# Spreading a row of B by fp32 transposes of one repeated column, and summing states by accumulating transposes, in a fused conv and selective-scan kernel

## What is computed

```
def step(h, inp):
    u_t, d_t, B_t, C_t = inp
    dA = jnp.exp(d_t[..., None] * A)
    h = dA * h + (d_t * u_t)[..., None] * B_t[:, None, :]
    y = jnp.einsum('bdn,bn->bd', h, C_t)
    return (h, y)
...
y = selective_scan(xs, delta, A, Bm, Cm, D)
y = y * jax.nn.silu(z)
return y @ out_proj_w.T
```

## Time and profile before

| | us |
|---|---|
| runs | 1001.99, 1002.55, 1007.24 (median 1002.55) |
| profiled execution | 998.73, span 996.6 |
| scan steps 0 to 63, first half | 256.6 to 479.9 |
| scan steps 0 to 63, second half | 732.8 to 954.5 |
| busy, share of the span | PE 85%, DVE 82%, ACT 56%, POOL 52% |

### The profile page before, as it was taken

One profiled execution on the slowest core, in us unless ns is written; L12 is line 12 of the kernel. 1 busy time (PEld: TensorE's weight loads), 2 busy tenths in 40 slices (PEclk: granted clock), 3 DMA queues, 4 the chain that ended last, 5 costly groups with the idle time before them and its releaser, 6 DMA issues. The chain is left out here.

```text
span 996.6 us, 8253 instructions
## 1 busy us (share of the span) xinstructions
PE 842.4 (85%) x2747; PEld 419.2 (42%) x2747; DVE 816.1 (82%) x670; ACT 555.7 (56%) x927; POOL 520.1 (52%) x240
## 2 busy tenths in 40 slices
PE   3999998976488898899999999797648889889985
PEld 2444443432144445455545444343214334544643
DVE  6899884476998998998999888447699999899852
ACT  3754231047569886787667333104765878678712
POOL 2016992110488685877211799311046869577740
PEclk8999999997799999999999999898968999999998
DMA  3000000002434453444100000000113544444411
GB/s 103 1 0 0 0 0 1 0 1 73 106 123 173 139 179 131 152 161 148 44 0 6 16 0 0 1 0 1 47 68 105 184 154 176 140 148 164 148 48 22
DMA packets 32870, 73.82 MB, mean 74 GB/s; under 512 B 15544, under 2 KB 15680, under 8 KB 32832
## 3 DMA queue, kind: packets, MB, share of 16 engines
q1 hardware_dynamic: 31424, 72.04, 21.5%
q0 software_dynamic: 320, 1.05, 0.5%
q10 hardware_dynamic: 1088, 0.26, 0.1%
HBM read 70.71 MB, written 2.62 MB: 74 GB/s over the span
## 5 line engine op out<-in xcount | busy, mean ns | idle before, releaser
L333 POOL TENSOR_TENSOR arena<-arena 128x1024 f32<-128x1024 f32 x128 | 305.3, 2391 | 106.6 <-DVE arena L1567 64.3
L1567 DVE TENSOR_TENSOR_SCAN arena<-arena,ps 128x1024 f32<-128x1024 f32 x128 | 289.4, 2280 | 15.9 <-POOL arena L333 8.3
L568 PE MATMUL ps<-arena,mat 128*128 128x512 f32 x512 | 251.7, 615 | 9.1 <-POOL arena L333 8.0
L808 ACT ACTIVATE arena<-arena,Amat 128x1024 f32<-128x1024 f32 x128 | 146.0, 1143 | 86.9 <-DVE arena L1567 83.4
L808 ACT ACTIVATE arena<-arena 128x128 f32<-128x128 f32 (+4 forms) x320 | 131.7, 480 | 106.4 <-DVE arena L1484 75.3
L568 PEld LDWEIGHTS ps<-arena,mat 128*128 128x128 f32 x512 | 95.1, 196 | 90.1 <-issue 67.2
L681 PE MATMUL ps<-arena,mat 128*128 128x512 f32 x240 | 106.3, 592 | 0.0
L535 PE MATMUL ps<-arena,sel 96*128 96x512 bf16 x148 | 48.0, 411 | 61.8 <-DVE arena L1567 52.4
L1562 DVE TENSOR_TENSOR ps<-arena,ps 128x1024 f32<-128x1024 f32 x74 | 89.5, 1210 | 5.7 <-PE ps L535 5.7
L808 ACT ACTIVATE arena<-ps 128x1024 f32<-128x1024 f32 (+2 forms) x58 | 53.6, 937 | 70.5 <-PE ps L409 20.7
L440 PE MATMUL ps<-arena,diag 128*128 128x512 f32 x180 | 80.5, 603 | 2.4 <-DVE ps L1397 2.4
(11 more groups left out here) (177 smaller groups left out, 1242.4 us busy)
## 6 DMA issues: line engine op xcount, KB each, us to landing
arena<-c_rows SPq DMA_DIRECT2D x128, 512.0 KB, 3.8
out<-arena SPq DMA_DIRECT2D x28, 64.0 KB, 2.2
xres<-x POOLq DMA_DIRECT2D x4, 256.0 KB, 5.3
xres<-x SPq DMA_DIRECT2D x4, 256.0 KB, 4.1
convw<-conv_w SPq DMA_DIRECT2D x1, 576.0 KB
c_rows<-ROWS SPq DMA_DIRECT2D x4, 128.0 KB, 1.9
mat<-mats SPq DMA_DIRECT2D x1, 448.0 KB, 3.9
inw<-in_w SPq DMA_DIRECT2D x1, 256.0 KB
```

Of the source, the lines that this page charges most:

```text
L333: tt(HC[s % 2], HS[s % 2], CB[s % 4], ALU.mult).then_inc(S("hc"), 1)
L568: last = mm(half(PS[3], n), ident, half(HC[s % 2], n), start=first, stop=True, skip_group_check=True)
L808: return nc.scalar.activation(out_, in_, func, bias=bias, scale=scale, accum_out=accum_out)
L1567: nc.vector.tensor_tensor_scan(HS[q], DA[q], PS[q][:, :], 0.0, ALU.mult, ALU.add).then_inc(S("scan"), 1)
```

## The change

It touches the Mamba block of both halves.

1. **No bf16 parts.** `first_part`, `middle`, `rest` and `last_part` are gone. B and C of a pair stand in 64 rows (`keep_rows` copies 64). Before the scan TensorE transposes pair 0's rows (`turn_first_rows`) and ScalarE keeps their B (`keep_first_b`) in `BT`. The other pair's B comes as before from `turn_rows`.
2. **A row of B by turns of a repeated column.** `b_rows` makes eight transposes of one fp32 column of `BT`, repeated 128 times, in place of two bf16 matmuls.
3. **State sums by accumulating turns.** For images 0 to 2 of a half (`TURNED`) `sum_of` makes eight transposes of 128x128 that accumulate in `PS[3]`, so y stands transposed; z is projected in that layout by eight matmuls of 128 columns. To give `out_proj` its operand, the gated y is transposed back (`turn_y`) and copied (`keep_y`). Image 3 is summed as before.
4. **More X steps.** From step 9 to 47 three of five are X steps (24 of 39 where 20 were); from 48 on every other one, as before: 31 of 64. The scaled blocks have a third buffer.
5. **Moved.** The pieces of pair 0's end go three steps later (output projection 33/34 to 36/37, last projection 44 to 47, centering 36 to 39, adding the block 46 to 49, and so on), and its result tile and store move. At the end of the first half two empty matmuls (`write_all`) open `PS[0]` and `PS[1]` before `first_tap`.

```diff
-            d["BCS"] = d["BCS"][:, 0:L // 2].bitcast(bf16)
+            d["TB"] = d["BCS"][:, L // 2:L]
...
+        def tb_block(i, n):
+            if i % 3 < 2:
+                return TB[i % 3][:, n * P:(n + 1) * P]
+            return D[n // 4]["TB"][:, n % 4 * P:(n % 4 + 1) * P]
...
-        X_STEPS = [s for s in range(9, SCANS - 1, 2)]
+        X_STEPS = [s for s in range(9, SCANS - 1) if (s % 5 in (0, 2, 4) if s < 3 * D_STATE else s % 2 == 1)]
         Z_STEPS = [s for s in range(SCANS) if s not in X_STEPS]
 
-        def rows_of(k, part):
-            at = 64 * k + 32 * part
-            return ROWS[at:at + 32, :]
+        def rows_of(k):
+            return ROWS[64 * k:64 * k + 64, :]
...
+        TURNED = [0, 1, 2]
...
                 for s in range(4, SCANS):
                     c_row(h, s)
-                    if s == SCANS - 3:
-                        store_out(h, 0)
+                store_out(h, 0)
                 store_out(h, 1)
...
+                wz = inw[:, 2 * P * b + P:2 * P * b + 2 * P]
+                if 2 * k + b in TURNED:
+                    for n in range(BLK):
+                        last = mm(blk(PS[2 * k + 1], n), blk(d["XNC"], n), wz, start=True, stop=True, skip_group_check=True)
+                else:
+                    for n in range(2):
+                        last = mm(half(PS[2 * k + 1], n), wz, half(d["XNC"], n), start=True, stop=True)
                 last.then_inc(S(f"z{k}"), 1)
...
-                at = 16 * (D_STATE * (j % 2) + s % D_STATE)
-                row = sel[:, at:at + 1]
-                for n in range(2):
-                    last = mm(half(PS[s % 2], n), row.to_broadcast([96, P]), half(D[j // 2]["BCS"][:, 0:L], n)[0:96, :], start=True, stop=True)
+                for n in range(BLK):
+                    column = BT[:, n, j, s % D_STATE:s % D_STATE + 1]
+                    last = nc.tensor.transpose(blk(PS[s % 2], n), column.to_broadcast([P, P]), ident)
                 last.then_inc(S("bb"), 1)
...
-                transposes(TB[i % 2], PS[s % 2]).then_inc(S("bb"), 1)
+                for n in range(BLK):
+                    last = nc.tensor.transpose(blk(PS[s % 2], n), tb_block(i, n), ident)
+                last.then_inc(S("bb"), 1)
...
+            def turn_first_rows(h):
+                pe.wait_ge(S("kept_c"), 2 * h + 1)
+                for n in range(BLK):
+                    last = nc.tensor.transpose(PS[1][:, 64 * n:64 * n + 64], rows_of(0)[:, n * P:(n + 1) * P], ident[0:64, 0:64])
+                last.then_inc(S("rows_turned"), 1)
...
                 pe.wait_ge(S("hc"), SCANS * h + s + 1)
-                for n in range(2):
-                    last = mm(half(PS[3], n), ident, half(HC[s % 2], n), start=first, stop=True, skip_group_check=True)
-                last.then_inc(S("sum"), 1)
-                if first:
+                if j in TURNED:
+                    for n in range(BLK):
+                        last = mm(blk(PS[3], n), blk(HC[s % 2], n), ident, start=first and n % 4 == 0, stop=True,
+                                  is_transpose=True, skip_group_check=True)
+                    last.then_inc(S("sum"), 1)
+                    if first:
+                        for n in range(BLK):
+                            mm(blk(PS[3], n), blk(two_images(j, "XS"), n), diagD[:, :], start=False, stop=True, skip_group_check=True)
+                else:
                     for n in range(2):
-                        mm(half(PS[3], n), diagD[:, :], half(two_images(j, "XS"), n), start=False, stop=True, skip_group_check=True)
+                        last = mm(half(PS[3], n), ident, half(HC[s % 2], n), start=first, stop=True, skip_group_check=True)
+                    last.then_inc(S("sum"), 1)
+                    if first:
+                        for n in range(2):
+                            mm(half(PS[3], n), diagD[:, :], half(two_images(j, "XS"), n), start=False, stop=True, skip_group_check=True)
+
+            def turn_y(h, j):
+                pe.wait_ge(S("y_read"), ONE + 4 * h + j + 1)
+                transposes(two_images(j, "SZ"), PS[2]).then_inc(S("y_turned"), 1)
+
+            def y_kept(h, j):
+                pe.wait_ge(S("y_kept"), len(TURNED) * h + j + 1)
...
                 pe.wait_ge(S("rx0"), 2 * h + 2)
-                pe.wait_ge(S("kept_c"), 2 * h + 1)
-                pe.wait_ge(S("split"), 2 * h + 1)
+                turn_first_rows(h)
+                pe.wait_ge(S("b_kept"), h + 1)
                 plain(pe)
                 b_rows(h, 0)
                 b_rows(h, 1)
                 dt_proj(h, 1, 1)
                 bc_proj(h, 1)
                 b_rows(h, 2)
-                pe.wait_ge(S("r11"), h + 1)
                 pe.wait_ge(S("kept_c"), 2 * h + 2)
                 for s in range(1, SCANS):
                     if s == 2 * D_STATE - 2:
-                        pe.wait_ge(S("split"), 2 * h + 2)
+                        pe.wait_ge(S("kept"), 5 * h + ROWS_TURNED)
                         plain(pe)
                     fill(h, s + 2)
+                    if s == SCANS - 1:
+                        if h + 1 < HALVES:
+                            pe.wait_ge(S("scan"), SCANS * h + s)
+                            write_all(PS[0])
+                        pe.wait_ge(S("ot"), 2 * h + 1)
+                        turn_y(h, 2)
...
+                        turn_y(h, 0)
+                    if s == 25:
+                        y_kept(h, 0)
                         turn_du(h, 2)
-                    if s == 28:
+                    if s == 30:
                         pe.wait_ge(S("kept"), turned(h, 2))
                         turn_du(h, 3)
-                    if s == 32:
+                    if s == 34:
                         pe.wait_ge(S("kept"), turned(h, 3))
-                        skip(0)
+                        turn_y(h, 1)
...
-                    if s == 33:
+                    if s == 36:
+                        y_kept(h, 1)
+                        skip(0)
                         out_proj(h, 0)
-                    if s == 34:
+                    if s == 37:
                         out_proj(h, 1)
-                    if s == 41:
+                    if s == 44:
                         xn2_channels(h, 0)
-                    if s == 44:
+                    if s == 47:
...
-                pe.wait_ge(S("ot"), 2 * h + 1)
+                if h + 1 < HALVES:
+                    pe.wait_ge(S("scan"), SCANS * (h + 1))
+                    write_all(PS[1])
+                y_kept(h, 2)
...
-            def first_part(h, k):
-                act.wait_ge(S(f"bc{k}"), h + 1)
-                av(rows_of(k, 0), PS[2 * k + 1][0:32, :], ACT.Identity)
-                av(D[k]["BCS"][0:96, :], PS[2 * k + 1][0:96, :], ACT.Identity).then_inc(S(f"bfpart{k}"), 1)
...
-            def middle(h, k):
-                d = D[k]
-                act.wait_ge(S(f"r1{k}"), h + 1)
-                av(d["BCS"][64:96, :], d["R1"][64:96, :], ACT.Identity).then_inc(S(f"bfpart{k}"), 1)
-                av(d["BCS"][32:64, :], d["R1"][32:64, :], ACT.Identity).then_inc(S(f"bfpart{k}"), 1)
...
-                av(BT_PAIRS, ps[:, :, :, 0:2 * D_STATE], ACT.Identity).then_inc(S("kept"), 1)
+                av(BT_PAIRS[:, :, 1, :], ps[:, :, 1, 0:2 * D_STATE], ACT.Identity).then_inc(S("kept"), 1)
+
+            def keep_first_b(h):
+                act.wait_ge(S("rows_turned"), h + 1)
+                ps = half(PS[1], 0).rearrange("p (k m) -> p k m", k=BLK)
+                av(BT_PAIRS[:, :, 0, :], ps[:, :, 0:2 * D_STATE], ACT.Identity).then_inc(S("b_kept"), 1)
 
             def scaled_input(h, s):
                 i, j = X_STEPS.index(s), s // D_STATE
                 if i == 0:
                     for r in range(2):
                         act.wait_ge(S(f"rows{r}"), 16 * h + 16)
-                if i == 1:
-                    act.wait_ge(S("split"), 2 * h + 2)
-                if i > 1:
-                    act.wait_ge(S("bb"), SCANS * h + X_STEPS[i - 2] + 1)
+                if i > 2:
+                    act.wait_ge(S("bb"), SCANS * h + X_STEPS[i - 3] + 1)
...
-                    last = av(blk(TB[i % 2], n), du_block(j, n), ACT.Identity, BT[:, n, j, s % D_STATE:s % D_STATE + 1])
+                    last = av(tb_block(i, n), du_block(j, n), ACT.Identity, BT[:, n, j, s % D_STATE:s % D_STATE + 1])
                 last.then_inc(S("scaled"), 1)
 
             def keep_rows(h, k):
                 act.wait_ge(S(f"bc{k}"), h + 1)
-                av(rows_of(k, 1), PS[2 * k + 1][96:128, :], ACT.Identity).then_inc(S("kept_c"), 1)
+                av(rows_of(k), PS[2 * k + 1][0:64, :], ACT.Identity).then_inc(S("kept_c"), 1)
+
+            def keep_y(h, j):
+                act.wait_ge(S("y_turned"), len(TURNED) * h + j + 1)
+                av(two_images(j, "SZ"), PS[2][:, :], ACT.Identity).then_inc(S("y_kept"), 1)
...
-                first_part(h, 0)
                 keep_rows(h, 0)
                 abs_x(h, 1, 0)
-                middle(h, 0)
```

(26 more changed lines are left out.)

81 lines of the change are left out of this document (36 added, 45 removed).

## The result

The changed kernel takes **989.76 us** (median of four runs, 987.52 to 989.93) against 1002.41 (1001.99 to 1007.24) before, a ratio of 0.986 with a 95% interval of 0.983 to 0.989. The profiled execution took 989.86 us, with a span of 987.7. That is 12.7 us less by the medians, but only 8.9 less than the profiled execution before, against which the sum was made and which was the fastest one seen then. The two scans take 445 of the 996.6 us before, so it is a little over half of the time, not two thirds, that lies outside of them.

A forecast was written before the change was run, and what follows sets the result against it. VectorE was the longest of four nearly full engines in steps 9 to 47. 2 x (-6.9 + 2.6 - 2.4 - 1.5) - 0.5 - 2.5 + 1.7 = -17.7 gave 985 us; own range 977 to 993.

The forecast's parts named there:

- The turns: On TensorE, eight turns take 0.88 us: a sum falls by 0.83, a Z step's fill rises by 0.45.
- Bf16 parts: VectorE's subtractions in steps 0 and 1 of each half, removed from a full engine: -2.4 us per half.
- Before the first scan: Start of each half up to its first scan, with copies and VectorE's last subtraction removed: -1.5 us per half.
- Steps 48 to 63: End of each scan, with plain sums of image 3, dearer Z fills and the moved `add_block`: +2.6 us per half.
- Steps 26 to 47: VectorE loses two multiplications, `add_block` and some idle time: -6.9 us in each half, from 76.8 to 69.9.
- Steps 9 to 25: ScalarE ends the first half's stretch at 55.5 us, -0.5; the second half's takes 51.7, -2.5.
- The changeover: Between the halves, the second `write_all` stands behind the sum of step 62 on TensorE: +1.7 us.
- The tail: After the second half: no change if step 63's product covers `turn_y` and `keep_y`, otherwise they show as 2 us.
- The clock at half in turned steps: Rival: TensorE at half clock in turned steps makes steps 9 to 47 longer, 1062 us in all; chance 0.09.
- ScalarE as the bound: Rival: ScalarE bounds steps 9 to 47, costing all but 2 us of 26 to 47's gain; 995 us, chance 0.14.
- the sentence of the Trainium skill that the prediction quoted: It says "HAM K=8/8 doesn't engage for transpose-mode", by which TensorE's clock would be at half for all turned steps.

## Why the prediction was right, and where it wasn't

The time was forecast at 985 and came out at 989.8, in its own range of 977 to 993. The direction and the order of size were right, and the sign was right in all stretches but two. The sum against the profiled execution was -17.7, and -8.9 was measured. The medians differ by 12.7, because that execution of the kernel before was a fast one: part of the agreement in the total, some 4 us, is luck.

- **The turns.** Eight accumulating turns (line 586) and eight turns of a repeated column (line 544) take 0.88 us from start to start, as taken. VectorE made 4.45 us less work of steps 26 to 47, as counted.
- **Bf16 parts.** -2.4 per half were forecast for steps 0 to 8, -2.5 and -2.7 measured. A removal on a full engine was worth its time there.
- **Before the first scan.** -1.5 forecast, -2.6 measured in the first half, and this is luck too. The projection before the last causal convolution ran at half clock before and at full clock after (TensorE, before, then after), which is 1.8 us:

```profile
234.71 3.75 PE L505 MATMUL ps<-arena,inw 128*128 128x512 f32 x4 [3.88 <-DVE arena L1531]
```

```profile
233.80 1.95 PE L510 MATMUL ps<-arena,inw 128*128 128x512 f32 x4 [2.62 <-DVE arena L1567]
```

  It began 0.9 us sooner and not 2, since ScalarE's `abs_x`, on which it hangs by way of VectorE, now waits 0.90 us for TensorE. From that convolution's start (L1513, after L1559) to the scan it took 18.1 us before and 18.2 after, though VectorE's last subtraction (1.22 us) was gone: ScalarE makes the Exps behind the copy of B, and VectorE waits 0.81 and 0.41 us for it:

```profile
248.57 1.23 DVE L1582 TENSOR_TENSOR arena<-arena 128x1024 f32<-128x1024 f32 x1 [0.81 <-ACT arena L857]
...
251.46 1.28 DVE L1567 TENSOR_SCALAR arena<-ps,vecs 128x1024 f32<-128x1024 f32 x1 [0.41 <-ACT arena L857]
```

  With that copy behind the Exps it is 16.7.
- **Steps 48 to 63.** +2.6 forecast, +2.0 measured. Turned sums are worth 2.4 us there, by the backlog at scan 48, where I had counted 0.8 for the one at the stretch's start. Without them it is 4.45 us, where my sum without that 0.8 gives 3.4: the fills and `add_block` cost 1.0 us more than I counted.
- **Steps 26 to 47: -6.9 forecast, -4.8 measured.** This is the step that failed. I let 2.4 of 6.9 us of idle time go and kept the rest. The 2.4 did go, but 2.3 came back at step 36, where `keep_y(1)` waits for `turn_y(1)` with a scaled input and a decay behind it. I had priced exactly this at step 25, and at step 36 had counted only the copy's busy time and found ScalarE's sum below VectorE's. Moving the copy gave back 1.6 of it.
- **Steps 9 to 25.** ScalarE as the end of this stretch in the first half was forecast at 55.5 us; it took 54.5, with ScalarE busy 51.2 (94%), 2.3 less than I had counted. In the second half I expected 51.7 and the idle time as before, and got 54.3. 1.15 us of that goes with a longer fall of the clock: the five kernels with these steps whose mean was 0.97 there took 53.2, the four with 0.94 took 54.3 to 54.5. Most of the rest is idle time: before the scans VectorE waits 3.6 us where it waited 2.3, for GpSimd 2.2 (1.6 before) and for ScalarE 1.1 (0.4 before).
- **The changeover.** +1.7 forecast, and 3.2 measured: from the last scan's end to the first Sobel sum (L1373 before; L1417 after) it took 3.3 us, now 6.5. The sum stands between, as forecast, but also `keep_y(2)` between the two first taps (timeline of the changed kernel):

```profile
471.01 1.12 ACT L857 ACTIVATE ps<-arena,vecs 128x1024 f32<-128x1024 f32 x1 [2.64 <-PE ps L452]
472.07 1.00 ACT L857 ACTIVATE arena<-ps 128x1024 f32<-128x1024 f32 x1
...
474.04 1.12 ACT L857 ACTIVATE ps<-arena,vecs 128x1024 f32<-128x1024 f32 x1 [0.97 <-PE ps L452]
...
477.19 1.29 DVE L1417 TENSOR_TENSOR arena<-arena 128x1088 f32<-128x1088 f32 x1 [2.41 <-ACT arena L857]
```

- **The tail.** 0 forecast, +3.8 measured. The gate waits 1.55 us longer (6.24 for 4.69), since TensorE comes to the end with a backlog (steps 60 to 63 hold `keep_x3`, the second DCT and eight-turn fills); the other 2.2 us is the clock behind waits of 0.68 and 1.18 us, which the unchanged tail has in some runs.
- **The rivals.** The clock at half in turned steps didn't come: it was 1.00 and 0.95 over steps 9 to 25 and 26 to 47 of the first half, 0.94 and 0.95 of the second. ScalarE as the bound came in part: at two places, by its order, rather than all through by its load. That is why other orders, and a few unused products against falls of the clock, gave 15.6 us and more.

## What to carry to other kernels

When work moves from a full engine to one that is nearly full, a sum of busy times doesn't tell what is gained. For every new wait on the receiving engine, list what is queued behind it, and move the waiting instruction behind that work before anything else is changed. Compare variants by stretches cut at the same instructions of their traces: medians of runs that spread by 5 us hid differences of 1.5 us that the stretches showed to 0.1. But look at the granted clock of each stretch first: where it differs, the stretch can differ by 1 us (steps 9 to 25) to 6 us (start to first scan) between runs of the same instructions, and a gain read there may be the clock's.

## What the runs showed of the hardware

Transposes alone brought TensorE's clock back. After 4.93 us without work it stood at half, and with nothing but transposes on the engine it was full again (timeline of TensorE, changed kernel):

```profile
395.96 1.94 PE L552 MATMUL ps<-mat,arena 128*128 128x128 f32 x8 [4.93 <-DVE arena L1603]
397.70 1.92 PE L586 MATMUL ps<-mat,arena 128*128 128x128 f32 x8
399.40 1.48 PE L544 MATMUL ps<-mat,arena 128*128 128x128 f32 x8
400.72 1.04 PE L586 MATMUL ps<-mat,arena 128*128 128x128 f32 x8
```

At half clock eight turns take 1.94 us, at full clock 1.04 with their end (0.88 to the next). So the sentence of the Trainium skill that the prediction quoted (TensorE: Matmul & The Clock Gate, part 4) isn't borne out by fp32 transposes here, plain or accumulating.

The same instructions behind the same wait found the clock full in one run and at half in another: 1.95 and 3.75 us behind 3.24 us of idle time, 2.98, 4.67 and 5.73 us for the 13 products of the tail. In this kernel that is worth up to 6 us before the first scan (253.99 and 260.10 us with the same program up to there) and 3.5 in the tail. It is likely most of the spread from run to run, but each kernel has only one profile, so that isn't shown. With unused products at five such places six runs of one kernel lay within 4.5 us and five of another within 1.3, where the kernel before spread by 7.0 and 5.4 in the same two sessions (and the changed kernel, in its four runs, by 2.4).
